# All plans in a new order, and each norm's and each gamma's rows of two sequences fetched by one broadcast DMA over 128 partitions instead of two over 64

## What is computed

```python
def layer0(x, cond):                              # x (64, 64, 512), cond (64, 512)
    h = x * rsqrt(mean(x**2, -1) + EPS) * (w * (1.0 + cond @ tw.T))[:, None, :]     # "gain" rows, one per sequence
    x = x + attention(h, rope, 8 query heads, 1 key/value head) @ Wo.T
    h = ...                                       # the same norm with its own gain rows
    return x + (silu(h @ Wg.T) * (h @ Wu.T)) @ Wd.T

def layer1(x, cond):
    ada = silu(cond) @ Wada.T + bada              # 6 rows of 512 per sequence
    gamma1, gamma2, scale1, scale2, shift1, shift2 = ada
    h = ln(x) * (scale1 + 1.0) + shift1           # "mod" rows: scale and shift, 1024 numbers per sequence
    x = x + attention(h, q and k of unit length, 16 heads) * gamma1     # "gamma" rows
    h = gelu_tanh((ln(x) * (scale2 + 1.0) + shift2) @ Wfc1.T + bfc1)
    return x + (h @ Wfc2.T + bfc2) * gamma2
```

## Time and profile before

| | us |
|---|---|
| median of 3 executions (lowest, highest) | 2560.11 (2558.06, 2566.29) |
| the profiled execution | 2554.55 |
| its span, first to last instruction | 2552.8 |
| TensorE busy in it | 2449.8 |
| mean granted clock of TensorE | 0.985 |
| one block of layer 0 / of layer 1 | 153.3 to 155.3 / 147.5 to 157.2 |
| TRANS | 197.4 |

### The profile page before, as it was taken

How to read it: one execution, slowest core, us unless ns; L and a number is a source line. 1 busy time by engine, 2 the same in 40 slices (tenths; PEclk the granted TensorE clock), 3 DMA queues, 4 the chain that set the end, 5 groups by cost and what they waited for, 6 DMA issues and landing times.

```text
span 2552.8 us, 46385 instructions
## 1 busy us (share of the span) xinstructions
PE 2449.8 (96%) x17878; PEld 1169.3 (46%) x17878; DVE 1422.2 (56%) x2062; ACT 912.4 (36%) x1496; POOL 1050.4 (41%) x943
## 2 busy tenths in 40 slices
PE   7799999999999999999999899999999999999999
PEld 4344444444444444444444444444444444444444
DVE  5674351524415244351874876848667586876842
ACT  3343221322313122231442643626344352634532
POOL 2342231322323233231552554646556464655633
PEclk7899999999999999999999999999999999999999
DMA  7752423323132231424334525252441524334230
GB/s 180 211 149 65 104 46 86 62 50 92 35 98 52 61 84 30 106 44 143 100 93 131 155 49 143 54 126 63 103 106 41 143 62 100 96 77 120 50 92 29
DMA packets 311504, 231.81 MB, mean 91 GB/s; under 512 B 227718, under 2 KB 238342, under 8 KB 311308
## 3 DMA queue, kind: packets, MB, share of 16 engines
q1 hardware_dynamic: 311308, 228.89, 35.8%
HBM read 124.08 MB, written 18.75 MB: 56 GB/s over the span
## 4 chain that ended last, share of the span: by engine, by line
PE 59%; POOL 16%; issue 12%; DVE 8%; ACT 3%; DMA 2%; SPq 1%; POOLq 0%; ACTq 0%; DVEq 0%
PE ps_m L1882 33%; PE ps_abef L1882 16%; POOL inner L1248 4%; PE ps_c L1882 3%; POOL scratch L1278 3%; POOL scratch L1274 3%; POOL scratch L1222 2%; POOL scratch L1284 1%; PE ps_d L1882 1%; DVE scratch L1845 1%; PE ps_abef L2105 1%; DMA inner<-tw_t 1%; DVE weights L1571 1%; ACT scratch L1505 1%; POOL x_attn L1287 1%
## 5 line engine op out<-in xcount | busy, mean ns | idle before, releaser
L1882 PE MATMUL ps_m<-h_mlp,weights 128*128 128x512 f16 x3168 | 736.4, 384 | 24.9 <-issue 8.5
L1882 PE MATMUL ps_m<-weights,inner 128*128 128x512 f16 x3072 | 679.3, 379 | 0.0
L1248 POOL TENSOR_TENSOR inner<-scratch,inner 128x512 f16<-128x512 f32 x256 | 322.4, 1264 | 489.8 <-ACT inner L1421 488.8
L1882 PEld LDWEIGHTS ps_m<-h_mlp,weights 128*128 128x128 f16 x3168 | 305.0, 99 | 395.2 <-issue 38.6
L1882 PEld LDWEIGHTS ps_m<-weights,inner 128*128 128x128 f16 x3072 | 298.1, 98 | 352.5 <-issue 0.2
L1882 PE MATMUL ps_abef<-h_mlp,weights 128*128 128x512 f16 x1440 | 329.0, 379 | 0.0
L1222 POOL TENSOR_TENSOR scratch<-scratch 128x512 f16<-128x512 f32 x120 | 163.1, 1359 | 340.2 <-ACT scratch L1374 340.2
L1882 PEld LDWEIGHTS ps_abef<-h_mlp,weights 128*128 128x128 f16 x1440 | 137.7, 98 | 165.6 <-issue 4.2
L1421 ACT CAST inner<-scratch 128x512 f16<-128x512 f32 x256 | 156.0, 613 | 121.8 <-DVE scratch L1716 64.4
L1374 ACT CAST scratch<-scratch 128x512 f16<-128x512 f32 x120 | 73.8, 615 | 334.3 <-DMA h_mlp<-scratch 189.3
L1845 DVE SCALAR_TENSOR_TENSOR scratch<-scratch 128x512 f32<-128x512 f32 x128 | 125.1, 978 | 61.2 <-ACT scratch L1510 61.2
(11 more groups left out here) (172 smaller groups left out, 3190.9 us busy)
## 6 DMA issues: line engine op xcount, KB each, us to landing
scratch<-mod SPq DMA_DIRECT2D x128, 256.0 KB, 4.0
x_mlp<-x_attn SPq DMA_DIRECT2D x64, 256.0 KB, 2.4
weights<-gamma SPq DMA_DIRECT2D x128, 128.0 KB, 3.1
scratch<-scratch SPq DMA_DIRECT2D x128, 128.0 KB
scratch<-gain SPq DMA_DIRECT2D x112, 128.0 KB, 3.0
x_attn<-x SPq DMA_DIRECT2D x32, 256.0 KB, 2.7
x_mid<-x_mlp SPq DMA_DIRECT2D x32, 256.0 KB, 2.2
x_attn<-x_mid SPq DMA_DIRECT2D x32, 256.0 KB, 2.9
```

The costliest lines, as they stand in the source:

```text
L1248: nc.gpsimd.tensor_tensor(inner[:, 1, j, :], src, inner[:, 0, j, :], ALU.subtract).then_inc(L.m_lo, 1)
L1882: ins = nc.tensor.matmul(o, left(a, k), right(b, k), start=(first and n == 0), stop=(last and n == len(order) - 1), skip_group_check=True)
```

## The change

It has two parts. First, the numbers of all plans are new, and with them the order of the stages on every engine. Of the tables only two lines are shown here; what the new order is at two places follows below. Second, `seq_pair` replaces `seq_rows`: the source of a fetch is now both rows at once, as a pattern (2 sequences, 64 repeats, 512 or 1024 numbers), and one DMA writes all 128 partitions. The semaphores of norms and gammas then rise by 16 per tile instead of 32.

```diff
 STEADY1_AT = {
-    "fetch1": tiles([-153.29, 15.37, 48.57, 167.04], 1),
...
+    "fetch1": tiles([-186.48, 0.66, 24.21, 204.33], 1),
...
-            def seq_rows(ap, it, t, b):
-
-                return ap.rearrange("(n s) d -> n s d", n=NBLK)[bass.ds(it, 1), 2 * t + b, :]
+            def seq_pair(ap, it, t):
+
+                two = ap.rearrange("(n s) d -> n s d", n=NBLK)[bass.ds(it, 1), 2 * t:2 * t + 2]
+                return two.rearrange("o s d -> (o s) d").unsqueeze(1)
...
             def fetch0(it, kind, t):
...
-                for b in range(2):
-                    row = seq_rows(gain0_dram[int(kind[4]) - 1], *block_of(it, t), b)
-                    sp.dma_start(gain_row[SEQ * b:SEQ * (b + 1), :], row.to_broadcast([SEQ, D])).then_inc(L0.tables, 16)
+                rows = seq_pair(gain0_dram[int(kind[4]) - 1], *block_of(it, t))
+                sp.dma_start(gain_row, rows.to_broadcast([2, SEQ, D])).then_inc(L0.tables, 16)
...
             def fetch1(it, kind, t):
...
-                for b in range(2):
-                    row = seq_rows(mod1_dram[int(kind[4]) - 1].rearrange("s k d -> s (k d)"), *block_of(it, t), b)
-                    dst = rows_t[SEQ * b:SEQ * (b + 1)].rearrange("p k n -> p (k n)")
-                    sp.dma_start(dst, row.to_broadcast([SEQ, 2 * D])).then_inc(L1.tables, 16)
+                rows = seq_pair(mod1_dram[int(kind[4]) - 1].rearrange("s k d -> s (k d)"), *block_of(it, t))
+                sp.dma_start(rows_t.rearrange("p k n -> p (k n)"), rows.to_broadcast([2, SEQ, 2 * D])).then_inc(L1.tables, 16)
...
             def gamma(L, which, dst, s, it, t):
-                for b in range(2):
-                    row = seq_rows(gamma_dram[which], it, t, b)
-                    sp.dma_start(dst[SEQ * b:SEQ * (b + 1), :], row.to_broadcast([SEQ, D])).then_inc(s, 16)
+                sp.dma_start(dst, seq_pair(gamma_dram[which], it, t).to_broadcast([2, SEQ, D])).then_inc(s, 16)
...
-                    dve.wait_ge(L1.tables, 32 * (m + 1))
+                    dve.wait_ge(L1.tables, 16 * (m + 1))
```

More of the change, by code:

```diff
@@ L110 @@
[L110 to L136, removed]
+    "rstd1": tiles([-79.57, -4.46, 33.51, 85.48, 283.81]),
+    "turn_x1": tiles([-52.37, 28.44, 52.77, 95.17]),
+    "scale1": tiles([-51.99, 28.87, 56.19, 91.19, 265.45]),
+    "stat1": tiles([-51.98, 28.88, 52.18, 107.57, 267.27]),
@@ L181 @@
[L181 to L190, removed]
@@ new lines @@
+    "qk_lo": tiles([-36.52, 32.94, 59.09, 80.64]),
+    "scale1": tiles([-35.16, 23.90, 26.89, 240.87], 1),
+    "fetch1": tiles([-34.56, 13.87, 26.58, 191.64], 1),
+    "m_hi": tiles([-27.69, 8.79, 27.51, 47.57, 51.04, 56.77, 65.34, 77.05, 98.60, 106.20, 107.38, 119.54, 156.23,
+        170.16, 197.40, 208.45]),
+    "lo1": tiles([-14.67, 26.47, 50.11, 280.71], 1),
+    "spread": tiles([4.29, 48.89, 71.51, 113.41]),
+    "qk_hi": tiles([8.01, 38.57, 51.50, 91.22]),
+    "turn": tiles([10.20, 39.40, 56.95, 108.35]),
@@ new lines @@
+    "p_hi": tiles([36.23, 53.76, 82.39, 127.40]),
+    "c_hi": tiles([43.06, 63.88, 95.75, 143.03]),
+    "mix": tiles([48.19, 60.04, 102.25, 133.67]),
+    "add": tiles([49.93, 76.00, 123.49, 162.56]),
+    "fetch2": tiles([51.05, 58.07, 132.99, 175.22]),
+    "rstd2": tiles([51.14, 110.04, 139.67, 200.67]),
+    "stat2": tiles([51.86, 99.60, 215.78, 266.20]),
+    "scale2": tiles([52.25, 120.57, 167.32, 171.73]),
+    "out": tiles([52.38, 65.71, 125.70, 151.96]),
+    "lo2": tiles([68.76, 130.53, 179.41, 200.89]),
@@ L200 @@
+    "hi2": tiles([81.15, 202.08, 219.66, 266.88]),
+    "tables": tiles([130.17], 3),
+    "flip2": tiles([130.59, 148.44, 178.51, 197.41]),
+    "store": tiles([141.75, 170.91, 192.35, 231.67]),
+    "y": tiles([157.45, 167.75, 234.09, 443.20]),
+    "down": jobs(4, 16, [157.95, 158.23, 161.92, 166.40, 170.39, 170.52, 170.94, 182.66, 182.88, 185.02, 185.86,
[5 rows of a table added]
+    "hand": tiles([159.97, 185.53, 204.16, 276.54]),
+    "next": tiles([196.70, 205.90, 232.58, 288.41]),
 }
 SETUP0 = [
-    (-75.94, "load", "ada4"), (-67.41, "sin", 0), (-65.45, "ada", "g0"), (-47.90, "ang", 0), (-46.73, "ang", 1),
@@ new lines @@
+    "stat2": tiles([79.71, 110.70, 192.68, 221.32]),
+    "scale2": tiles([81.13, 136.58, 195.60, 229.37]),
+    "fetch2": tiles([81.42, 85.67, 137.78, 200.42]),
+    "hi2": tiles([93.68, 206.08, 252.63, 285.60]),
+    "lo2": tiles([93.80, 159.45, 212.81, 242.00]),
+    "flip2": tiles([163.24, 165.72, 217.84, 230.07]),
+    "store": tiles([187.13, 203.82, 240.45, 307.52]),
+    "down": jobs(4, 16, [189.87, 193.48, 195.01, 195.61, 199.11, 199.61, 199.78, 200.49, 201.99, 203.23, 205.65,
[5 rows of a table added]
+    "hand": tiles([191.16, 224.51, 259.26, 356.09]),
@@ new lines @@
+    "hi1": tiles([-10.84, 22.95, 58.71, 296.05], 1),
+    "scale1": tiles([-5.81, 21.39, 41.31, 248.46], 1),
+    "inv_k": tiles([-2.79, 48.80, 69.55, 111.79]),
+    "projv": tiles([-0.76, 29.38, 56.30, 88.45]),
+    "spread": tiles([2.75, 59.78, 86.36, 126.26]),
+    "lo1": tiles([3.87, 19.83, 56.01, 302.77], 1),
+    "v_lo": tiles([4.04, 37.60, 70.69, 109.06]),
+    "flip1": tiles([6.18, 52.83, 82.95, 229.42], 1),
+    "unit_q": tiles([7.24, 48.88, 81.83, 115.12]),
+    "unit_k": tiles([7.82, 51.01, 84.99, 116.69]),
@@ new lines @@
+    "fetch2": tiles([79.05, 101.34, 129.65, 164.36]),
+    "lo2": tiles([82.35, 144.12, 161.06, 232.88]),
+    "down": jobs(4, 16, [88.75, 89.53, 90.44, 93.16, 93.42, 97.60, 99.14, 104.87, 105.09, 105.10, 107.88, 109.31,
[4 rows of a table added]
+    "hi2": tiles([97.59, 121.72, 184.24, 239.79]),
+    "d": tiles([114.03, 155.66, 181.26, 272.53]),
+    "flip2": tiles([121.71, 138.54, 184.48, 216.77]),
+    "y": tiles([123.76, 160.35, 278.03, 329.88]),
+    "store": tiles([133.61, 141.43, 216.82, 233.95]),
+    "hand": tiles([150.70, 160.62, 236.24, 241.23]),
@@ L403 @@
+    "next": tiles([179.15, 179.99, 267.41, 283.36]),
 }
 LAST1_AT = {
[L405 to L410 removed]
```

391 lines of the change are left out of this document (185 added, 206 removed), and 119 rows, old and new, of tables (LAST1_AT, SETUP_START0, SETUP_START1, SETUP_TRANS).

## The result

| | us |
|---|---|
| median before (4 executions beside the changed kernel) | 2562.23 (2558.06 to 2566.29) |
| median after (4 executions) | 2953.13 (2946.65 to 2956.34) |
| ratio | 1.152, 95% interval 1.149 to 1.155 |
| predicted | 2800, range 2620 to 2980 |
| profiled execution, its span | 2954.86, 2953.0 |

The changed kernel is 391 us slower. The direction and the mechanism were as forecast; the size was forecast at 240.

A forecast was written before the change was run, and what follows sets the result against it. Merged fetches on 2 of 16 DMA engines were to stretch layer 1's serial fetch chain, stalling TensorE (96% busy before): 2554.55 + 217 (layer 1) + 15 (TRANS) + 7 (layer 0) + 3 (LAST1) = 2796.6, stated as 2800 us, range 2620 to 2980.

The forecast's parts named there:

- The number of engines: Merged fetches: the source's outermost dimension sets the engines sharing a DMA, so 2 of 16, with 64 partitions' rows on each.
- The price of a fetch: Merged fetch on 2 engines: mod 14.3 us (64 packets at 0.177 plus 3.0), or 17.7 at 0.229; gamma and gain 8.8.
- The load of the two engines: Layer-1 block: the two engines get 175 us of work, more than its 150.8 by 24; with 0.229 a packet 202.
- its +15: TRANS: eight mod fetches each 9.8 us later, most with cover, put at +15 us (0 to +40).
- The chain of four fetches: Layer 1, one buffer for all mod fetches: four fetches with scales between grow from 48.4 to 81.1 us, +33 per chain.
- the step from a scale's end to the issue of the next fetch: In the layer-1 chain: 0.8 us from each scale's end to the next fetch's issue, four times 3.1.
- The first of the two ways forecast: Layer 1: `flip2` of tile 3 lands late, queued behind a fetch of 11.3 us on its two engines, delaying TensorE.
- VectorE held at a `scale`: Second way to TensorE: a waiting `scale` holds `arg` and `gelu` behind it, with two banks between them and TensorE.
- layer 0: Eight gain fetches a block each 5.2 us later, TensorE never having waited: +1 a block, +7 us (0 to +21).
- +217: Layer 1: seven pairs of neighbouring blocks each hold a chain, 7 x 31 us (+33 less 2 for waits inside longer ones).
- B: Rival: two engines but hidden, only the fetch already waited for grows, 10 us per block: 2630 us, chance 0.09.
- C: Rival: the merged DMA is spread over 16 engines, so the order decides, 24 us faster: 2536 us, chance 0.08.

The follow-up runs named there:

- the series over 2, 4, 8 and 16: Changed kernel with rows stored 1, 2, 4 or 8 times in HBM, so the source's outermost dimension is 2, 4, 8 or 16: 2953, 2610, 2550 and 2529 us.
- the order alone: Changed kernel with the old fetches put back (new order, two DMAs over 64 partitions per tile): 2503.88 us, ratio to before 0.979; repeat 2507.62.
- 8 copies: Changed kernel with gain, mod and gamma rows stored 8 times in HBM, so one DMA has 16 outermost: 2528.54 us, ratio to before 0.989.

## Why the prediction was right, and where its size was off

**The number of engines.** Right, and shown twice: the share of 0.13 in stretches of fetches alone, and the series over 2, 4, 8 and 16. The step from one DMA with 8 outermost down to 2 held.

**The price of a fetch.** Right in sum, 14.3 us forecast and 13.45 measured. The packet was dearer in the forecast (0.177 us) than it is (0.158).

**The load of the two engines.** With 0.158 and 5.2 per gamma it is 36.3 + 81 + 42 = 159 us a block, in place of 175. A block took 194.3, so the load is not the bound; the chain is. (For TRANS the forecast took 7 us of old mod fetches off the load. By its own numbers, 14.7 for eight mod fetches and 3 for four gammas, it should have been about 18; its +15 did not hang on it.)

**The chain of four fetches.** Forecast 81.1 us, measured 88.4: from 2058.3 (end of `scale2` of tile 2) to the `scale1` of tile 2 of the next attention at 2146.68. The term that was too small is the step from a scale's end to the issue of the next fetch, put at 0.8 us each and 3.1 in all. The four steps took 11.2, 0.2, 9.3 and 0.2, together 20.9 us. Against this the four fetches took 62.7 us (13.45, 17.07, 13.11 and 19.05), where the forecast had 73.2 with what queues ahead of them (57.2 + 10 + 6), so one error hid a part of the other.

The step of 11.2 comes from the merge: in the order alone it is 0.2. SP was held until 2062.3 by the transpose issued at 2052.72, and then 4.8 us more by its wait for the store of 2062.49, which the hand-over of a tile (`x_mlp<-x_attn`) has to see landed; it issued the fetch at 2069.52. I counted the DMAs ahead as work on the engines, and left out that SP itself stands still at an issue while the queues of the two engines are long. The step of 9.3 does not come from the merge: the order alone has 9.6 us there, from 1829.61 to the issue at 1839.17, and the kernel before 9.7 (1860.20 to 1869.90). SP has other waits and issues to pass ahead of this fetch. The trace of before had this step already, and the forecast put it at 0.8.

The chain and the rest of a layer-1 block, first in the changed kernel, then in the order alone:

```profile
1952.34:2058.30 105.96, 102.15 (x1038) 51.08 (x1039) 77.05 (x106) 51.05 (x78) 55.80 (x39) 0.96 0.46 57
2058.30:2146.68 88.38, 47.72 (x292) 21.46 (x290) 21.37 (x38) 16.50 (x27) 22.27 (x21) 0.78 0.80 88
...
1712.06:1814.01 101.95, 101.74 (x1138) 51.55 (x1139) 77.66 (x107) 50.96 (x79) 57.33 (x40) 1.00 0.31 68
1814.01:1858.46 44.45, 40.83 (x192) 18.29 (x190) 21.50 (x39) 16.22 (x27) 21.31 (x20) 1.00 0.61 155
```

Of the 47.9 us that the merge adds to a block (194.3 against 146.4), 43.9 are in the chain. Against the kernel before the chain grew by 40.0 us (88.4 against 48.4), where the forecast had 32.7; seven of them are 280, of the 287.5 measured in layer 1.

**How the delay reaches TensorE.** The first of the two ways forecast is right: `flip2` lands late (184.3 us of waits in layer 1). So is a late `flip1`, which it did not name (74.9). The second, VectorE held at a `scale`, shows in layer 1 not through `arg`, `gelu` and the two banks but through L1741 (L1745 of before), which stands behind a `scale` too (39.8 us in eight waits). In TRANS the second way is the larger one: TensorE waited there 52.9 us for four of its lines (L1717, L1705, L1712, L1789), and VectorE 56.0 us for mod fetches.

**What the forecast left out.** First, TensorE's clock. In the stall of 28.75 us the granted clock fell to 0.50 (the row 2091 to 2101), 1.2 GHz. Over layer 1 it is 0.88, and TensorE is busy 46.3 us longer than with the same order and two DMAs (1046.8 against 1000.5); the rest of the 326.9 us is idle time, 302.2 against 21.6. The forecast had the clock in neither direction. That it made the kernel slower is not shown: the extra busy time, 6.9 us a block, lies in the stretch of the chain (47.72 against 40.83), where TensorE is idle for 40.7 us besides. Second, layer 0: put at +7 because TensorE had no idle time there, measured +51 against before, +43 against the order alone, and +47 for the whole kernel by merging the gains alone. TensorE waited there seven times for a DMA that `mix` needs (12.4 us), four times for L1717 on VectorE (8.7) and six times for `flip1` (5.6), where all its waits were 0.9 us in the order alone. "TensorE never did" wait said nothing of how much cover there was, nor of the other DMAs that queue behind a gain fetch; the forecast took the cover for ample. Its upper bound of 21 was too low as well. TRANS, forecast +15 with an upper bound of 40, came out at +71.9.

**The range.** That 2953 lies in it is in part luck. Its upper end is worked out from the load of the two engines at 0.229 us a packet; the packet took 0.158, and the load did not set the time.

Layer 1 was forecast at +217 and came out at +287.5; against the order alone it is +327. The order's own gain was forecast at 24 for its rival and is 54; by the stretches 39 lie in layer 1, where 24 were forecast, 5 in TRANS and 7 in start and layer 0 together, which I had not costed at all.

**The rivals.** B (hidden but for one fetch) would have been 2630 and is excluded by the blocks of 194. C was wrong for this kernel, but its reasoning for the order was right in sign: with the fetches spread, the new order is faster than before by 1.1% (8 copies) to 2.2% (two DMAs). The advice of the Trainium skill ("DMA: Bandwidth & Descriptors", "Rules for kernel authors") to take one transfer over 128 partitions instead of two over halves is, by these runs, worth next to nothing here where the DMA has 16 engines (2.9 us in seven layer-1 blocks), and costs 449 us where its source begins with a dimension of 2. The other rule of the same page of the Trainium skill, that the slowest dimension sets the number of engines, agrees with 0.13 of 16 engines for 2.

The version that beats both kernels is the new order with two DMAs per tile: 2503.88 us, 2.1% faster than before and 15% faster than the changed kernel.

## What to carry to other kernels

Look at the outermost dimension of both patterns of a DMA before merging two into one: here a leading 2 left 2 of 16 DMA engines, and the queue of these two then delayed DMAs of other kinds issued behind it (the transposes landed after 8.2 us in the median, 3.3 in the order alone). Price such a change not only by the landing of the DMA itself but by the issuing engine, which stands still when those queues are long, and take its steps between two DMAs of a chain from the trace, one by one. And when a change has two parts, run them apart: here one was worth 2% and was hidden under the other.

## What the runs showed of the hardware

- A DMA with 2 outermost moves 49 to 52 GB/s on two engines; a packet of 4 KB takes 0.158 us there, against 0.229 where a pair of fetches is spread over all 16.
- A transpose that SP issued in 1.24 us in the median before took up to 12.6 us to issue, behind a gamma and a mod fetch on the same two engines. The issue of a fetch can be held too, as the second of these two gammas, behind a mod and a gamma (the row is both issues):

```profile
1919.60 7.89 SPq L993 DMA_DIRECT2D weights<-gamma  x2
```

- With DMA transposes behind fetches on two engines the profile's share of the 16 engines counts waiting as busy: 50.1% of the engines' time with transposes, 27.9% with plain DMAs of the same size, and 6.65 times the engines' time in one stretch of 2 us.
